# Attention on one core: one visit to TensorE's column tiles for a pair of steps, with two banks for scores and four for maxima

## The reference

```python
# x: (2, 2048, 512), 16 heads of 32
q, k, v = heads(ln(x) @ Wq.T), heads(ln(x) @ Wk.T), heads(ln(x) @ Wv.T)
q, k = rope(q), rope(k)
scores = einsum('bhqd,bhkd->bhqk', q, k) / sqrt(32)
attn = softmax(where(causal, scores, -inf))
ctx = einsum('bhqk,bhkd->bhqd', attn, v)
x = x + ctx.reshape(B, S, D) @ Wo.T
```

## Time and profile before

| | |
|---|---|
| median of three runs | 1747.59 us |
| profiled execution | 1746.13 us, span 1744.1 us |
| mean granted clock of TensorE | 0.963 |
| TensorE matmuls busy | 1633.1 us (94%) |
| VectorE | 1146.7 us (66%) |
| GpSimd | 881.5 us (51%) |
| ScalarE | 768.8 us (44%) |

### The profile page before, as it was taken

One profiled execution on the slowest core, in us unless ns is written; L12 is line 12 of the kernel. 1 busy time (PEld: TensorE's weight loads), 2 busy tenths in 40 slices (PEclk: granted clock), 3 DMA queues, 4 the chain that ended last, 5 costly groups with the idle time before them and its releaser, 6 DMA issues. The chain is left out here.

```text
span 1744.1 us, 32355 instructions
## 1 busy us (share of the span) xinstructions
PE 1633.1 (94%) x9440; PEld 995.4 (57%) x9440; DVE 1146.7 (66%) x2662; ACT 768.8 (44%) x1544; POOL 881.5 (51%) x558
## 2 busy tenths in 40 slices
PE   6999999489999999999999999999999986999998
PEld 4888887245455455545455554545545424777775
DVE  5666664568777767766777776777777505666654
ACT  3222221034565556555555555555655653222221
POOL 1332323335667767666667666766667771112111
PEclk9999999579999999999999998999999997999999
DMA  5556644961134134125116116107102004222311
GB/s 181 191 183 222 217 163 145 225 132 32 26 73 100 26 75 97 26 53 113 26 26 146 26 24 148 26 8 161 29 8 80 7 13 139 73 72 72 129 64 48
DMA packets 103220, 157.19 MB, mean 90 GB/s; under 512 B 10545, under 2 KB 43825, under 8 KB 100401
## 3 DMA queue, kind: packets, MB, share of 16 engines
q1 hardware_dynamic: 93296, 136.10, 28.9%
q10 hardware_dynamic: 9792, 19.40, 3.0%
HBM read 96.23 MB, written 58.72 MB: 89 GB/s over the span
## 5 line engine op out<-in xcount | busy, mean ns | idle before, releaser
L751 ACT ACTIVATE a_probs<-a_st 128x512 f32<-128x512 f32 (+3 forms) x1280 | 593.7, 537 | 462.7 <-PE a_st L667 457.8
L624 POOL TENSOR_TENSOR a_pair<-a_probs 128x1024 f32<-128x1024 f32 (+2 forms) x320 | 613.8, 1939 | 226.8 <-ACT a_probs L751 213.1
L770 DVE TENSOR_REDUCE a_part<-a_mx 128x1 f32<-128x512 f32 x768 | 504.8, 683 | 181.9 <-PE a_mx L655 179.5
L655 PE MATMUL a_mx<-a_k_stack,a_q_stack 96*128 96x512 f32 (+3 forms) x1280 | 489.5, 396 | 47.4 <-DMA a_q_stack<-qk_scratch 24.9
L667 PE MATMUL a_st<-a_q_stack,a_k_stack 98*128 98x512 f32 (+3 forms) x1280 | 490.9, 400 | 14.2 <-issue 6.8
L667 PEld LDWEIGHTS a_st<-a_q_stack,a_k_stack 98*128 98x128 f32 x1280 | 244.8, 193 | 286.1 <-issue 162.4
L655 PEld LDWEIGHTS a_mx<-a_k_stack,a_q_stack 96*128 96x128 f32 x1280 | 250.0, 196 | 140.6 <-DVE a_part L770 53.0
L774 DVE CUSTOM_DVE_ANT_0 a_mx<-a_mx,a_mask 128x384 f32<-128x384 f32 (+3 forms) x512 | 249.5, 497 | 89.6 <-PE a_mx L655 88.5
L211 POOL TENSOR_TENSOR p_rot<-p_mul 128x1024 f32<-128x1024 f32 x32 | 90.7, 2835 | 213.2 <-DVE p_mul L406 213.2
L982 POOL TENSOR_TENSOR f_x<-f_x,f_bias 128x512 f32<-128x512 f32 x32 | 41.4, 1325 | 230.2 <-DVE f_xn L1175 230.2
L609 POOL TENSOR_SCALAR_AFFINE_SELECT a_probs<-a_probs 128x512 f32<-128x512 f32 x128 | 80.7, 635 | 144.2 <-ACT a_probs L751 144.0
(11 more groups left out here) (134 smaller groups left out, 1587.0 us busy)
## 6 DMA issues: line engine op xcount, KB each, us to landing
a_q_stack<-qk_scratch SPq DMA_DIRECT2D x96, 256.0 KB, 5.2
a_k_stack<-qk_scratch SPq DMA_DIRECT2D x21, 1024.0 KB, 12.6
qk_scratch<-p_rot_hi SPq DMA_DIRECT2D x32, 512.0 KB, 3.1
qk_scratch<-p_rot_lo SPq DMA_DIRECT2D x32, 512.0 KB, 3.9
v_scratch<-p_v_st SPq DMA_DIRECT2D x32, 256.0 KB, 7.0
ctx_scratch<-a_ctx_st SPq DMA_DIRECT2D x32, 256.0 KB, 2.4
f_ctx<-ctx_scratch SPq DMA_DIRECT2D x8, 1024.0 KB, 8.9
f_x<-in_x SPq DMA_DIRECT2D x8, 1024.0 KB, 7.9
```

What stands on the lines that cost most here:

```text
L624: pool.tensor_tensor(pair[:, p % 2, h:h + 2, q0:TT], probs[:, s % RING, h:h + 2, q0:TT], probs[:, (s + 1) % RING, h:h + 2, q0:TT], ALU.add ...
L655: mm = pe.matmul(mx_ps[k % MX_BANKS][:, 0:width], q_stack[0:96, t, h, qi * P:(qi + 1) * P], k_stack[par][0:96, h, c * TT:c * TT + width], ...
L751: act.activation(probs[:, s % RING, h, q0:TT], st_ps[:, (HG * s + h) % BANKS, q0:TT], ACT.Exp, scale=SCORE_SCALE).then_inc(exp_done, 1)
L770: dve.tensor_reduce(found, mx_ps[k % MX_BANKS][:, :], AX.X, ALU.max).then_inc(max_done, 1)
```

## The change

The bank counts become 2 for scores and 4 for items. TensorE's `group` issues, for pair p, all eight scores of steps 2p+2 and 2p+3 in one run with the pair's items spread evenly between them, then the values of both steps, then the sums. The last lines of the run issue what is left of the items. No instruction is added or removed, and the other engines' streams change in the bank numbers alone.

```diff
-        BANKS, MX_BANKS = 3, 3
+        BANKS, MX_BANKS = 2, 4
...
             def group(g, par, use, next_use, first, last):
                 for p in range(NPAIR):
                     items = [(n, k) for n, k in items_of_pair(p, first) if not (n and last)]
-                    middle = (len(items) + 1) // 2
-                    for half, due in enumerate((items[:middle], items[middle:])):
-                        s = 2 * p + 2 + half
-                        for i in range(max(HG, len(due))):
-                            if i < HG and s < NSTEP:
-                                scores(g, par, s, i)
-                            elif i < HG and not last:
-                                scores(g + 1, 1 - par, s - NSTEP, i)
-                            if i < len(due):
-                                n, k = due[i]
-                                item(g + n, (par + n) % 2, next_use if n else use, k)
-                        values(g, par, 2 * p + half)
+                    issued = 0
+                    for i in range(2 * HG):
+                        while issued < len(items) and issued * 2 * HG <= i * len(items):
+                            n, k = items[issued]
+                            item(g + n, (par + n) % 2, next_use if n else use, k)
+                            issued += 1
+                        s, h = 2 * p + 2 + i // HG, i % HG
+                        if s < NSTEP:
+                            scores(g, par, s, h)
+                        elif not last:
+                            scores(g + 1, 1 - par, s - NSTEP, h)
+                    for n, k in items[issued:]:
+                        item(g + n, (par + n) % 2, next_use if n else use, k)
+                    values(g, par, 2 * p)
+                    values(g, par, 2 * p + 1)
                     sums(g, p)
```

## The result

The changed kernel takes 1792.95 us (median of four runs, 1789.96 to 1795.69) against 1745.88 (four runs): 1.0269 times the time before, 95% interval 1.0242 to 1.0296. It is slower by 2.7%, where 1790 us had been forecast. The profiled execution took 1789.96 us.

The account below looks back on a forecast made before the run. TensorE's instruction stream was taken as the bound. Six steady turns +30, last turn +2.5 and +9, first turn +3.8 and -1, sum +44 on 1746.1 us, gave 1790 us, range 1775 to 1806.

Parts of the forecast that it names:

- the score loop: A score and its exponential through one of two score banks: 1.19 us a loop, adding 21 us a turn.
- Switching: TensorE entering and leaving a visit to the column tiles: about 0.30 us each, one fewer per pair, 48 us off.
- the 6.0 us a turn: Switching time on TensorE forecast to go in each turn (four heads, twenty pairs of steps).
- Fronts of 4.71, 4.95, 4.5 and 3.2: TensorE's issue between two visits, in us: full scores with at most 8 maxima, with 9 or 10, 512/384 wide, 256/128 wide.
- Four item banks: Four banks for maxima, spread evenly: VectorE's waits put at nothing, bounds none to some 2 us a turn.
- the 10 of the prediction's bookkeeping: Waits in each turn of the kernel before, 10 us by the prediction's count, forecast to go.
- The loop edges of VectorE: Pair behind a loop edge, where VectorE sat 2.68 us idle: a possible loss of some 2 us a turn.
- the turn's bookkeeping: A steady turn summed from fronts, tiled work, sums and leaving: 136.9 us against 131.9 before, +5.0.
- the six steady turns: The six middle turns at +5.0 us each: +30 us.
- The last turn: First ten pairs, with maxima, +2.5 us; the nine fronts after, without maxima, +9 us.
- The first turn: Pairs 5 to 19 +3.8 us; first five pairs, a little less starving with four banks, -1 us.
- The second rival: Score loop shorter, without 0.10 us per waiting score: 48 us less, 1742 to 1746 us, no change; chance 0.10.

Follow-up runs that it names:

- the cut visit: Changed kernel with each pair's last item held back and issued between the values of the two steps, cutting the visit in two: 1866.57 us.
- The halved exponentials: Each exponential works on the second half of its columns only: 1721.13 us in the changed kernel, 1738.51 us in the kernel before.
- the first experiment: Changed kernel's order (one visit a pair, items spread) with the old three score and three item banks: 1766.56 us, 1.0133 times the kernel before.

## Why the prediction was right, and where it was off

**The time** was 1793 for 1790, within the forecast's own 1775 to 1806, and the mechanism was the forecast's own, the score loop. By its own steps:

**Switching**: 0.30 us forecast, 0.34 in the cut visit. The uncut one takes 2.71 to 2.72 for 2.74. That the 6.0 us a turn come off the path beside the loop is bookkeeping that no pair of runs shows: with two score banks the new order is worth 0.3 us a turn (829.9 for 831.8 us in six), since the loop sets the fronts in either order.

**The score loop**: 1.19 us forecast and seen in the full fronts. Fronts of 4.71, 4.95, 4.5 and 3.2 were forecast; in the sixth turn the six full ones with at most eight items have 4.59 to 4.72, the six with nine or ten 4.71 to 4.96, those of 512 and 384 wide scores 4.50 to 4.72, and those of 256 and 128 wide ones 3.08 to 3.26 away from the loop edge. The halved exponentials showed that it is this loop.

**Four item banks**: VectorE's waits put at nothing; 1.5 us in 800 remain of the 55.0 before, and those are some 9 a turn, near the 10 of the prediction's bookkeeping. The loop edges of VectorE even gained: pair 0 of the fifth turn went from 6.77 to 5.96 us. That was left out of the sum, and so was the 0.8 us by which the turn's bookkeeping was high (136.9 for 136.1): the six steady turns took 24.5 us more and not 30 (from the end of the first turn's last visit, 511.61 to 1316.99 before, 514.44 to 1344.29 after).

**The last turn**: first half +3.8 for +2.5. Second half +13.0 for +9 (from the end of pair 9's visit to the end of pair 17's: 58.7 for 45.7 us), and 4.2 of that is the clock, which I had held at 1.00. Its full pairs are 7.19 us for the 7.2 forecast wherever the clock held.

**The first turn**: +2.8 for +2.8. The sum is 44.1 for 44: the steady turns' 5.5 too many and the last turn's 5.3 too few met. That the total came so near is partly luck: the mechanism was the forecast one, but its terms were off by 5 us in either direction.

**The second rival** had the waiting scores without their 0.10: scores 2, 4 and 6 are listed at 0.50 in the front shown. The page "TensorE: Matmul & The Clock Gate" of the Trainium skill (section "Architectural detail: the array is 16× 32×32, not 1× 128×128") says that TensorE's queue can pull weight loads ahead of matmuls in flight. The trace agrees where nothing waits (the load of the score at 848.28 starts at 848.05), and not behind a wait: no load of a waiting score begins before the exponential that it waits for has ended (849.36 and the others).

**What the prediction didn't see**: it asked whether the gain of the order or the loss of the bank would win, as if the order had 0.30 us a pair to give once the loop was out of the way. With three item banks the first experiment refutes that: the longer visit starves VectorE and costs more than it saves. At neither tried division of the six banks is the whole kernel faster with one visit in every pair. What three score banks with four item banks would do is open: with those of values and sums that would be nine banks, and there are eight.

## What to carry to other kernels

Gathering work of one kind into longer runs saves the switches between, but each consumer of the other kind then needs banks enough to bridge the longer run, and time enough to catch up after it: count, for every ring, the loop through one buffer (here 0.53 + 0.66 us) over the number of buffers, and compare it with the producer's rate. Where a loop sets the pace, making its neighbours' instructions narrower is worth nothing, and making the loop's own slower step shorter is worth its full length there, until the next bound; an ablation of that step in both kernels tells a latency bound from a throughput bound. Choose the order pair by pair rather than for all: here a list of six pairs in twenty with one visit beat both none and all.

## What the runs showed of the hardware that I had not expected

TensorE's granted clock fell within the attention stage after fronts in which it issued little or waited once: three visits in the last turn at 0.66 to 0.70 of the clock in 5 us stretches, 1.1 to 1.7 us lost each, and in the first experiment some 13 us more over the run than in the kernel before, one of those visits behind a single wait of 1.18 us. It isn't regular: behind the same wait in other turns the clock stayed at 1.00. Extra matmuls of no use, put into the last turn's waits, went with a clock of 1.00 in the one trace taken, and cost nothing.
